# Local attention: scores on eight tiles of the array and in four half banks, one bank for the turned probabilities, and a new order of the engines' queues around them

## What is computed

```python
def _L1_attn_ref(x, w_qkv, b_qkv, w_out, b_out):
    NUM_HEADS, HEAD_DIM, WINDOW = 16, 16, 33
    PAD = WINDOW // 2
    qkv = (x @ w_qkv.T + b_qkv).reshape(b, s, NUM_HEADS, 3 * HEAD_DIM).transpose(0, 2, 1, 3)
    q, k, v = jnp.split(qkv, 3, axis=-1)
    idx = jnp.arange(s)[:, None] + jnp.arange(WINDOW)[None, :]
    k_win, v_win = pad(k)[:, :, idx, :], pad(v)[:, :, idx, :]
    scores = jnp.einsum('bhsd,bhswd->bhsw', q, k_win) / jnp.sqrt(HEAD_DIM)
    attn = jax.nn.softmax(scores, axis=-1)
    ctx = jnp.einsum('bhsw,bhswd->bhsd', attn, v_win)
    return ctx.transpose(0, 2, 1, 3).reshape(b, s, 256) @ w_out.T + b_out

x = x + _L1_attn_ref(_layernorm(x), ...)
```

## Time and profile before

| | |
|---|---|
| median of 3 runs | 1601.21 us (1599.86 to 1601.43) |
| the profiled execution | 1595.64 us, of which the span of the profile is 1593.8 |
| busy in the span | PE 99%, PEld 72%, DVE 76%, ACT 61%, POOL 46% |
| TensorE's granted clock | 1.00 of full speed in every stretch |
| local attention | its first scores start at 1263.82, the FFN behind it is alone on PE from 1474.27 |

### The profile page before, as it was taken

One profiled execution on the slowest core, in us unless ns is written; L12 is line 12 of the kernel. 1 busy time (PEld: TensorE's weight loads), 2 busy tenths in 40 slices (PEclk: granted clock), 3 DMA queues, 4 the chain that ended last, 5 costly groups with the idle time before them and its releaser, 6 DMA issues.

```text
span 1593.8 us, 46566 instructions
## 1 busy us (share of the span) xinstructions
PE 1570.9 (99%) x17333; PEld 1144.7 (72%) x17334; DVE 1210.6 (76%) x2549; ACT 966.5 (61%) x1816; POOL 735.2 (46%) x678
## 2 busy tenths in 40 slices
PE   9999999999999999999999999999999999998999
PEld 4665559999666776666555669999566777877676
DVE  7777777888676667768776568887788878888876
ACT  5354555777487767754434337776476576674765
POOL 3342242444256566553433324444254667767343
PEclk9999999999999999999999999999999999999999
DMA  8133223334311211003210123333432022221001
GB/s 268 57 106 92 91 94 100 119 119 119 93 28 29 39 26 26 1 1 104 84 50 30 39 82 107 119 119 103 99 78 41 11 81 68 66 66 42 28 27 53
DMA packets 91468, 115.81 MB, mean 73 GB/s; under 512 B 9456, under 2 KB 76688, under 8 KB 91344
## 3 DMA queue, kind: packets, MB, share of 16 engines
q1 hardware_dynamic: 70992, 71.21, 15.3%
q0 software_dynamic: 20352, 42.88, 9.5%
HBM read 66.14 MB, written 47.90 MB: 72 GB/s over the span
## 4 chain that ended last, share of the span: by engine, by line
PE 88%; DVE 6%; ACT 2%; issue 2%; DMA 1%; POOL 1%; SPq 0%; DVEq 0%; ACTq 0%; POOLq 0%
PE ps L2103 20%; PE ps L2104 20%; PE ps L2105 20%; PE ps L2338 3%; PE ps L2389 3%; PE ps L2388 3%; PE ps L2339 3%; PE ps L2119 2%; PE ps L2302 2%; PE ps L2628 2%; PE ps L2662 2%; PE ps L2490 1%; PE ps L2640 1%; PE ps L2450 1%; PE ps L2515 1%
## 5 line engine op out<-in xcount | busy, mean ns | idle before, releaser
L805 POOL DMA_INDIRECT routed<-work x142 | 139.2, 980 | 209.4 <-ACT work L1072 204.5
L2103 PE MATMUL ps<-xt_hi,wsh 128*128 128x512 f16 x508 | 192.8, 380 | 2.6 <-DVE work L1599 1.9
L2104 PE MATMUL ps<-xt_lo,wsh 128*128 128x512 f16 x508 | 192.7, 379 | 0.0
L2105 PE MATMUL ps<-xt_hi,wsh 128*128 128x512 f16 x508 | 192.7, 379 | 0.0
L1003 ACT ACTIVATE work<-ps 128x512 f32<-128x512 f32 x128 | 76.1, 597 | 164.7 <-PE ps L2105 164.4
L1599 DVE SCALAR_TENSOR_TENSOR work<-ps,work 128x512 f32<-128x512 f32 x128 | 88.1, 689 | 74.1 <-ACT work L1003 71.6
L2103 PE MATMUL ps<-wsh,work 128*128 128x256 f16 x512 | 139.6, 273 | 0.7 <-DVE work L1528 0.6
L2105 PE MATMUL ps<-wsh,work 128*128 128x256 f16 x512 | 139.6, 273 | 0.0
L2104 PE MATMUL ps<-wsh,work 128*128 128x256 f16 x512 | 139.6, 273 | 0.0
L1099 ACT ACTIVATE work<-ps,cols 128x512 f32<-128x512 f32 x120 | 82.6, 690 | 54.7 <-PE ps L2339 43.5
L2388 PE MATMUL ps<-w2q,work 128*128 128x256 f16 x512 | 113.4, 273 | 0.0
(11 more groups left out here) (296 smaller groups left out, 5073.6 us busy)
## 6 DMA issues: line engine op xcount, KB each, us to landing
work<-expert_x SPq DMA_DIRECT2D x142, 129.0 KB, 2.0
later<-values SPq DMA_DIRECT2D x32, 256.0 KB, 3.5
yg<-in_w_later SPq DMA_DIRECT2D x9, 498.0 KB, 3.5
w1q<-in_w_later SPq DMA_DIRECT2D x9, 498.0 KB, 3.7
yg<-in_w SPq DMA_DIRECT2D x16, 256.0 KB, 3.4
values<-wsh SPq DMA_DIRECT2D x8, 512.0 KB, 3.7
expert_x<-work SPq DMA_DIRECT2D x30, 129.0 KB, 3.3
yg<-routed SPq DMA_DIRECT2D x7, 512.0 KB, 3.6
```

The lines of the kernel that those rows point to most:

```text
L805: nc.gpsimd.indirect_dma_start(routed[:, :], bass.IndirectOffsetOnAxis(m.homes[:, i:i + 1], 0), m.t_y[:, i % 4, :], None).then_inc(s[f"til ...
L2103: nc.tensor.matmul(out_, a[0], b[0], start=start, stop=False)
L2104: nc.tensor.matmul(out_, a[0], b[1], start=False, stop=False)
L2105: return nc.tensor.matmul(out_, a[1], b[0], start=False, stop=stop)
```

## The change

- `scores` of 24 of the 32 tiles (`wide`: tiles 1 to 3 of sequences 1 to 6, tile 0 of sequences 2 to 7) alternate the column half with f, so that eight tiles of 32 by 64 are used and not four, and write the first halves of banks 2 to 5, one bank for each pair. The window addition reads these four half banks, and `context` reads the turned probabilities from the places to which this moves them.
- `turn` of most tiles uses bank 6 alone, in two halves: the second half waits until ACT has copied the first. PE does the first half where the whole turn stood, the second after the scores of tile t + 1 (at t = 2 after the transposes of the normed rows). ACT's copy of the second half stands ahead of the exponentials, but behind them at t = 0.
- At t = 2 the transposes of the normed rows go into banks 2 and 3. They come after `context` and wait for the window addition of tile 2; the scores of tile 3 come after both halves of the values and wait for both halves of the new rows. `xt_lo_of` stands behind the sums.
- On DVE at t = 0 the first `take` stands between the window addition and the maximum. On ACT `normed_rows` is split in two, with `ct_hi` and the keys between.

The core of the diff (the waits for the first values' rows, `is_first(g) or half and g == 1`, are left out):

```diff
+        WSCORE = 2
+        def wide(g, t):
+            return 1 <= g < NSEQ - 1 if t else 2 <= g
+        def turned_amid(g, t):
+            return 1 <= g < NSEQ - 1 if t < 2 else g < NSEQ - 2
+        def turn_bank(g, t, b):
+            return 6 if turned_amid(g, t) else WTURN + b
...
 # ACT, step
                     for t in range(TPS):
+                        g2, _, t2 = turns_back(g, u, t, 2)
+                        turned(g2, t2, (0,))
                         if t == 1:
-                            normed_rows(g)
+                            normed_rows(g, range(2))
+                        ct_hi(*turns_back(g, u, t, 3))
                         if t == 2:
-                            xt_hi_of(g + N0(n) + 2, u, WXT_AMID)
-                        if has_turn(g, t, 2):
-                            g2, _, t2 = turns_back(g, u, t, 2)
-                            turned(g2, t2)
-                        if has_turn(g, t, 3):
-                            ct_hi(*turns_back(g, u, t, 3))
+                            xt_hi_of(g + N0(n) + 2, u, WSCORE)
                         if t == 1:
                             queries_keys(g + 1, 1 - u, (KT,))
+                        if t:
+                            turned(g2, t2, (1,))
                         exps(g, t)
                         if t == 0:
+                            turned(g2, t2, (1,))
                             queries_keys(g + 1, 1 - u, range(KT))
                         elif t == 1:
+                            normed_rows(g, range(2, TPS))
                             queries_keys(g + 1, 1 - u, (KT + 1,))
...
 # DVE, step
-                        softmax(g, t)
                         if t == 0 and g >= 2:
-                            take(g - 2, lambda: sums(g - 1, 1 - u, 3))
+                            softmax(g, t, lambda: take(g - 2, (0,)))
+                            sums(g - 1, 1 - u, 3)
+                            take(g - 2, (1,))
+                        else:
+                            softmax(g, t)
                         if t == 0:
                             shift(g)
-                        if t == 2:
-                            xt_lo_of(g + N0(n) + 2, u, WXT_AMID)
                         if has_turn(g, t, 1) and t:
                             sums(*turns_back(g, u, t, 1))
+                        if t == 2:
+                            xt_lo_of(g + N0(n) + 2, u, WSCORE)
...
 # PE, scores
-                                dims, out_ = slice(pair * 32, (pair + 1) * 32), slice(pair % 2 * 64, (pair % 2 + 1) * 64)
+                                dims, bank, c = slice(pair * 32, (pair + 1) * 32), 3 + pair // 2, pair % 2
+                                if wide(g, t):
+                                    at, bank, c = blk * KB, WSCORE + pair % 2 * 2 + pair // 2, (pair + f) % 2
                                 ins = nc.tensor.matmul(
-                                    ps[out_, 3 + pair // 2, at:at + KB], ...
+                                    ps[c * 64:(c + 1) * 64, bank, at:at + KB], ...
...
 # PE, turn
+                    for b in halves:
+                        if has_turn(g, t, 1) and (b == 0 or turned_amid(g, t)):
+                            pe.wait_ge(s["pt_copied"], (g * TPS + t) * 2 + b)
+                        for j in range(4 * b, 4 * b + 4):
+                            ins = nc.tensor.transpose(ps[:, turn_bank(g, t, b), (j % 4) * P:(j % 4 + 1) * P],
...
 # PE, step
                     for t in range(TPS):
+                        g2, _, t2 = turns_back(g, u, t, 2)
+                        turn(g2, t2, (0,))
+                        context(*turns_back(g, u, t, 3))
                         if t == 2:
-                            pe.wait_ge(s["qk_copied"], (g + 2) * 2 * KT - 1)
-                            transposes(g + N0(n) + 2, b=WXT_AMID)
-                        if has_turn(g, t, 2):
-                            g2, _, t2 = turns_back(g, u, t, 2)
-                            turn(g2, t2)
-                        if has_turn(g, t, 3):
-                            context(*turns_back(g, u, t, 3))
+                            pe.wait_ge(s["windowed"], g * TPS + t + 1)
+                            transposes(g + N0(n) + 2, b=WSCORE)
+                            turn(g2, t2, (1,))
+                            for part in range(2):
+                                rows_part(g, u, t, part)
+                            xt_ready(g + N0(n) + 2)
+                            scores(g, u, t + 1)
+                            continue
                         rows_part(g, u, t, 0)
                         if t < TPS - 1:
                             scores(g, u, t + 1)
                         else:
                             scores(g + 1, 1 - u, 0)
+                        turn(g2, t2, (1,))
                         rows_part(g, u, t, 1)
```

More of the change, by code:

```diff
@@ L1255, in exps, with turned @@
                     nc.scalar.activation(m.p[t], m.p[t], ACT.Exp, scale=AD ** -0.5).then_inc(s["exp_ready"], 1)
-                def turned(g, t):
-                    for b in range(2):
+                def turned(g, t, halves=range(2)):
+                    for b in halves:
                         act.wait_ge(s["pt_ready"], (g * TPS + t) * 2 + b + 1)
                         nc.scalar.activation(m.pt[:, t % 2, 4 * b:4 * b + 4].rearrange("p a b -> p (a b)"),
-                                             ps[:, WTURN + b, :], ACT.Copy).then_inc(s["pt_copied"], 1)
+                                             ps[:, turn_bank(g, t, b), :], ACT.Copy).then_inc(s["pt_copied"], 1)
                 def ct_hi(g, u, t):
@@ L1962, in win, with softmax @@
                 sc = ps[:, 3:5, :].rearrange("p a (b k) -> p (a b) k", k=KB)
-                def softmax(g, t):
+                def softmax(g, t, amid=None):
                     dve.wait_ge(s["sc_ready"], g * TPS + t + 1)
@@ L1992, in ct_lo, with take @@
                                             m.c_hi[:, u, :, sl], ALU.subtract).then_inc(s["ct_lo"], 1)
-                def take(g, between=None):
-                    dve.wait_ge(s["bias_added"], g + 1)
-                    for half in range(2):
-                        if half and between is not None:
-                            between()
+                def take(g, halves=range(2)):
+                    if 0 in halves:
+                        dve.wait_ge(s["bias_added"], g + 1)
+                    for half in halves:
                         dve.wait_ge(s["y_ready"], g * 2 + half + 1)
@@ L2607, in values_rows @@
                             pe.wait_ge(s["qk_copied"], (g + 1) * 2 * KT)
-                        if half or is_first(g):
+                        if is_first(g) or half and g == 1:
                             xt_ready(g + N0(n) + 1)
@@ L2630, in scores, with turn @@
                                     m.k[dims, u, f, key:key + KB], start=True, stop=True, skip_group_check=True)
                     ins.then_inc(s["sc_ready"], 1)
[L2633 to L2643 removed]
+                def turn(g, t, halves=range(2)):
+                    if 0 in halves:
+                        pe.wait_ge(s["norm_ready"], g * TPS + t + 1)
+                        if not has_turn(g, t, 1):
+                            pe.wait_ge(S[n - 1]["y_taken"], 2 * NSEQ + 2)
+                    for b in halves:
+                        if has_turn(g, t, 1) and (b == 0 or turned_amid(g, t)):
+                            pe.wait_ge(s["pt_copied"], (g * TPS + t) * 2 + b)
+                        for j in range(4 * b, 4 * b + 4):
+                            ins = nc.tensor.transpose(ps[:, turn_bank(g, t, b), (j % 4) * P:(j % 4 + 1) * P],
+                                                      m.p[t][:, 2 * j:2 * j + 2].rearrange("p a b -> p (a b)"), ident)
+                        ins.then_inc(s["pt_ready"], 1)
@@ L2660, in context @@
                             sl = slice(h * QB, (h + 1) * QB)
+                            at, from_ = j, sl
+                            if wide(g, t):
+                                at, group = blk * KT + h // 2, (f ^ h // 2) * 2 + h % 2
+                                from_ = slice(group * QB, (group + 1) * QB)
                             own = m.vz[u][:, t * BPT + blk].rearrange("p a (d e) -> p (a d) e", e=KT * 4)[:, :, f * 4 + h]
-                            ins = nc.tensor.matmul(ps[sl, context_bank(g, t), f * P + blk * QB:f * P + (blk + 1) * QB], own, m.pt[:, t % 2, j, sl],
-                                                   start=True, stop=True, skip_group_check=True)
+                            ins = nc.tensor.matmul(ps[sl, context_bank(g, t), f * P + blk * QB:f * P + (blk + 1) * QB], own,
+                                                   m.pt[:, t % 2, at, from_], start=True, stop=True, skip_group_check=True)
                     ins.then_inc(s["c_ready"], 1)
```

44 lines of the change are left out of this document (22 added, 22 removed).

## The result

The changed kernel takes **1607.74 us** (median of 6 runs, 1606.40 to 1609.12), the kernel before, beside it, 1601.32 (1599.86 to 1601.75): a ratio of 1.004 with a 95% interval of 1.003 to 1.005. It is slower, by 6.4 us; 1607.4 was predicted, with a range of 1598 to 1611.

A forecast was written before the change was run, and what follows sets the result against it. PE (99% busy) paced the kernel; the dependency loop would overtake it, 26.04 against 24.89 us. Five turns give 5.7, the start 0.44: +6.2 on 1595.64 profiled is 1601.8, plus 5.6 to the median: 1607.4 us, range 1598 to 1611.

The forecast's parts named there:

- The loop: Local attention's dependency cycle per sequence, scores through POOL's normalization to context: predicted to grow from 23.9 to 26.04 us.
- W3 to W0: DVE's stretch from the window addition of tile 3 to that of the next sequence's tile 0: 6.09 us.
- the way to the first W3: Stretch before the first window addition of tile 3, ahead of the five turns: predicted 0.44 us longer.
- (a): Rival on DVE: `shift` escapes POOL's lock and runs in 0.15 us; loop 24.5, 1599.5 us; chance 0.20.
- (c): Rival on the scores: eight tiles gain nothing, so the loop has 0.47 us more; 1610.6 us; chance 0.10.
- Part 1: Scores on eight tiles: 8 turns of the tiles instead of 16, 0.47 us less per block in 24 of 32.
- Part 2: Turn in two halves through bank 6: costs PE 0.12 us a sequence; first half's copy stays hidden.
- Part 3: Normed-row transposes in banks 2 and 3, before tile 3's scores: adds 0.88 and 1.32 us to the dependency cycle.
- the cover: 3.96 us of PE work from the transposes on, hiding new halves ready after 3.36; without it, scores would slip.
- Part 4: First take ahead of tile 0's maximum on DVE: delays POOL by about 0.5 us; `shift` still held, 1.8 us.
- the hold: DVE's `shift` kept waiting by the port lock until POOL's operation ends: 1.8 us in place of 1.29.
- (b): Rival: PE still sets the pace, a sequence takes 23.1 us; 1592.8 us; chance 0.12.

The follow-up runs named there:

- the run in two parts: Changed kernel with the scores of tiles 0, 1 and 2 issued in two parts of 32 records around the turn's second half: 1602.28 us, ratio 1.0042.
- the run with both edits: Changed kernel with `shift` ahead of tile 0's maximum and tile 3's scores between the two halves of the values: 1599.61 us, ratio 1.0018.
- scores between: Changed kernel with tile 3's scores between the two halves of the values instead of behind both: 1600.40 us, ratio 1.0026.
- The run with shift first: Changed kernel with `shift` moved behind the first take and ahead of tile 0's maximum: 1600.80 us, ratio 1.0027.
- the last run: Changed kernel with normed-row transposes ahead of the turn again, `shift` behind tile 0's maximum, tile 1's sums ahead of `xt_lo`: 1594.65 us, ratio 0.9991.

## Why the prediction was right, point by point

**The loop sets the pace and not PE: right, link by link.** Predicted and measured, from the rows after:

| link | predicted | measured |
|---|---|---|
| W3 to W0 | 6.09 | 5.93 (1370.81 to 1376.74) |
| W0 to POOL's subtraction | 3.04 | 3.00 (to 1379.74) |
| its two operations | 3.77 | 3.76 (to 1383.50) |
| to W1 | 0.27 | 0.28 (to 1383.78) |
| to the next subtraction | 2.54 | 2.54 (to 1386.32) |
| to the end of tile 0's normalization | 3.76 | 3.76 (to 1390.08) |
| PE, up to W3 | 6.57 | 6.81 (to 1396.89) |
| sum | 26.04 | 26.08 |

The shares of the whole: the loop was to give 5.7 us and gave 6.0 (1317.67 to 1448.12 is 130.45, before 124.44); the way to the first W3 was to give 0.44 and gave 0.9; the end was to give nothing and gave back 0.2. Sum 6.7 in the stage for 6.2 predicted. That the turn agrees to 0.04 us is in part luck: PE's link was 0.24 longer than predicted, and W3 to W0 0.16 shorter. Two sums of the rivals are 0.1 off: (a) is -1.6 and not -1.7, (c) 1610.7 and not 1610.6; nothing rests on them.

**Part 1 is the step that was mis-sized.** "0.47 us less per block" was 0.25: from first to last start 0.697 us in place of 0.943, next operation after 0.84 us in place of 1.09. What limits it was named rightly and stops holding half-way. Read start by start, a round of eight tiles (eight starts 7 ns apart, then 12 ns) takes 0.059 us, as long as a round of four did (four starts 7 ns apart, then 38). The records do not name their tile, but rounds of eight and of four fit the eight and the four tiles: a tile can be used again after 0.059 us, whatever lies between. Only the first round of a block takes longer, 0.107 us with eight tiles and with four, so this pace to the end would have given 0.44. After 32 records, though, most starts come 8 to 17 ns apart instead of 7 (the run in two parts), and that takes 0.19 back. The prediction named the bound ("64 starts must still be issued") and priced it at nothing. The rule of the Trainium skill, "TensorE: Matmul & The Clock Gate", section "Part 3: Packing small matmuls", which would have made the gain nothing, is not borne out here: tiles in one row strip overlapped in the context rows and in the new scores alike, and undoing part 1 cost 2.4 us. The rival (c), which rested on it, is out. The 0.22 us missing a turn is nearly all of the error in PE's link.

**Part 2, 0.12 us a sequence: about nothing by itself.** A turn of before without gaps is 24.78 us; four blocks of 0.25 less would be 23.8, which is what the run with both edits leaves. Of the 0.25 more in the changed kernel (24.05), 0.17 are the three times 0.055 us of its transposes behind waits; where the rest lies is not shown. The copy of the first half cost no wait of PE, as said.

**Part 3 is the largest culprit.** It was reckoned at 0.88 + 1.32 us of the loop. Undone, the ratio falls from 1.0042 to 1.0012, 4.8 us, though a block of eight tiles is given up for it (on one chip, 1597.79 beside the 1602.28 of the run in two parts, whose ratio is that of the changed kernel). The new halves kept up as predicted: `xt_lo` ends at 1395.27, the scores start at 1395.94 without a wait, and the wait for W2 cost nothing. What the prediction said would happen without the cover is what "scores between" then met.

**Part 4 and the hold: right, and the thin margin of 0.18 us held in each turn.** `shift` 1.75 us, five times (predicted 1.8). The take as a link is 0.48 us long and worth 0.3 us a turn. The prediction did not see that the take also frees PE's bank; behind the maximum, PE waited 0.93 us for it, and 1.45 where `shift` stood ahead of the maximum too.

**Rivals.** (a), hold missed, would have given -1.7 us against the kernel before. The run with shift first makes that case by force, and it stays 4.1 us slower (1600.80 beside 1596.70). Its working was wrong: it took the loop over tile 0 for the only one, and the normalization of tile 3 holds the loop at 25.25. The forecast itself did not suffer, since over tile 0 the chain is the longest. (b), PE still paces at 23.1, is out by the waits alone. The 3 us of waiting foreseen were 2.04, and at three turns, since PE's own work with these waits shrank to 24.05 and not to 23.1. (c) is told above.

**What stays open:** what the gaps are, and why they fall in one turn and not in the next. They fall in other blocks in each run and are 0.2 to 0.9 us long in the lists of waits. The kernel before has one too, which its list does not show: a block of scores of 1.36 us from first to last start in place of 0.943, in its turn of 25.18; no run here varied what could cause them. The Trainium skill, "Runtime: NRT & Kernel Launch", section "Instruction fetch mechanics", says that each engine's instructions arrive block by block by a queue of its own; no run here shows whether the gaps lie at such borders.

## What to carry to other kernels

Lay the links of a queue loop end to end beside the busiest engine's own work, before trusting a busy share of 99%: here 24.9 us of PE work stood over 23.9 of dependencies, and moves that cost no engine anything (transposes and half of the values ahead of a critical block of scores, 2.2 us, and a take ahead of a maximum, 0.5) made the loop 26.1. A stall is worth its length only where its chain is the longest: taking away a hold gave nothing in one kernel and 2.65 us in the other, and there a third of what its own chain promised, because the next chain stood only 0.83 us a turn below it. And before an instruction is moved, look up when each of its inputs is ready: `shift` ahead of its rstd cost 5 us.

## What the runs showed of the hardware

- f32 matmuls of 32x64 tiles, two records each, start 7 ns apart, and a round of four tiles or of eight takes 0.059 us (the first of a block 0.107). Tiles in the same row strip do overlap: eight records of 0.217 us, two to a strip by the order of the calls, start within 0.047 us.
- This lasts for about 32 records. The next 32 of a block start mostly 8 to 17 ns apart (0.43 us in place of 0.27), and an interruption of four transposes restores the pace.
- A 128x4 operation of DVE, 0.15 us where POOL is idle, takes up to 1.75 us beside a 1.90 us operation of POOL and ends with it. Issued just ahead of POOL's next operation it takes 0.17 us.
- Gaps in which PE waits for nothing shown turn into time only where they are longer than the waits behind them in the same turn. The changed kernel has 1.7 us of them in five turns, all 26.08 to 26.10 long; behind the last wait they show in full: with the waits gone, in the last run, turns of 24.40 stand beside ones of 24.73 and 25.17.
